# First attention of a gated cross-attention network: TensorE's groups put in another order within each sequence's eight ticks

## The chip, the cores and the metric

The kernel runs on one core of one Trainium2 chip. The metric is device time in microseconds (us) of one execution, smaller is better. Three executions were timed, and one more was profiled. A measurement of this kernel can tell a change of about 1% from none.

## What is computed

There are 64 sequences of 128 tokens and 256 channels, and a context of the same shape. Four layers follow each other: a first attention, a first feed-forward layer (ternary weights), a second attention and a second feed-forward layer. The change touches the first attention alone:

```python
qh, kh, vh = (z.reshape(B, S, 16, 16) for z in (layernorm(x), ctx, ctx))   # 16 heads of 16
s1 = einsum('bshe,bthe->bhst', qh @ wq1, kh @ wk1) / 4
s2 = einsum('bshe,bthe->bhst', qh @ wq2, kh @ wk2) / 4
attn = softmax(s1) - gain * softmax(s2)
o = einsum('bhst,bthe->bshe', attn, vh @ wv)
o = (o - mean(o)) / sqrt(var(o) + 1e-5)         # over each head's 16 channels
x = x + tanh(g_xattn[0]) * (o @ wo.T)
```

## The kernel before

The five engines run one program each, written out by hand. `Attention0.pe`, `act`, `dve`, `pool` and `sp` hold one loop each over ticks, eight to a sequence: `b, u = divmod(tick, 8)` (GpSimd's loop goes by whole sequences). Every engine executes its list strictly in order and waits on semaphores, so the place of a step in the list sets what stands behind it. `ahead(tick)` calls steps of the next layer, from tick 500 on.

One sequence b passes through these steps. The names of the program, the line on which the profile puts them and, for TensorE, the tile form of the matmul (contraction rows * output columns of the array) are:

- `turn_queries(b, half)`, L549, 128*128: four transposes of the normalised queries into bank 7. ScalarE's `q_stack` (L684) copies them out.
- `keys(p)`, L523, 64*128, and `values(p)`, L536, 128*128: once for each pair p of sequences, into banks 6 and 7. ScalarE's `k_high` (L664), VectorE's `rest_keys` (L757) and twelve DMAs of SyncE (`stack_keys`, two halves r of six) build the key stack; ScalarE's `values` (L670) builds `v_pad`.
- `maxima(b, u)`, L561, 48*128, u = 0 to 3: scores of four of the sixteen heads, two row tiles at once, into banks 0 and 1. VectorE's `find_max` (L764) reduces them. The next `maxima` waits for that (`max`).
- `max_rows(b)`, L510, 128*32: one transpose of the maxima into bank 6. ScalarE copies it (L690), and two DMAs of SyncE (L438) put it into the query stack as rows. `scores_t` waits for their landing (`s_mdma`).
- `scores_t(b, u)`, L574, 50*128: the transposed scores less the maxima, into banks 2 and 3. ScalarE's two `exponential`s (L695) read them; the next `scores_t` waits for both (`exp`).
- `weighted(b, u)`, L585, 128*32: weighted sums of the values, four column tiles at once, into bank 5. ScalarE's `out_t` (L700) copies each half of a sequence out.
- `back(b, hf)`, L602, 128*128: four transposes into bank 4. VectorE divides (L771, L774) and, after the second half, makes the `difference` (L781); GpSimd squares (L861), VectorE sums (`variance`, L786), GpSimd normalises (L867 to L871).
- `project(b)`, L612, and `project2(b)`, L619, 128*128: two transposes and two matmuls, again in bank 4; ScalarE's `normed_t` (L705) lies between them and VectorE's `add` (L791) ends the sequence.

Before, TensorE's list for one tick pair is: `maxima`, `weighted`, then (in u = 2) `max_rows`, and (u = 2, 4) a half of `turn_queries`; in the odd tick `scores_t`, then one of `back`, `project`, `back` with `values` or `keys`, `project2`. In the letters of the tile forms (M `maxima`, S `scores_t`, both with half the rows; W `weighted`, quarter columns; F full tile; K `keys`, half the rows) a sequence is

```
before:  M W | S F(back) | M W F(max_rows, turn) | S F(project) | M W F(turn) | S F(back, values) or F(back) K | M W | S F(project2)
after:   S M | W W F(project2) | S M | F(max_rows, turn, back) | S M (K) | W W F(project, values) | S M | F(turn, back)
```

The banks are the same in both: each group has one buffer in PSUM, so the next group of its kind waits for the engine that reads it.

Of the kernel before, what the change touches and what calls it, by code (L numbers as in the profile page):

```python
# [303 lines left out]
class Attention0:  # L304
# [77 lines left out]

    def stack_keys(self, w, p, r):

        s, k = self.s, p % self.NK
        w.wait_ge(s["k_lo"], 2 * p + r + 1)
        w.wait_ge(s["k_hi"], 2 * p + r + 1)
# [22 lines left out]
    def sp(self, w, ahead):  # L410
# [42 lines left out]
        for tick in range(self.START, self.END):  # L453
# [30 lines left out]
    def pe(self, w, ahead):  # L484
# [54 lines left out]
        def turn_queries(b, half):  # L539
# [5 lines left out]
            elif half == 0 and b % 2 and b + 1 < NSEQ:  # L545
# [7 lines left out]
        def maxima(b, u):  # L553
            n = 4 * b + u
            w.wait_ge(s["q_st"], 2 * b + 2)
# [35 lines left out]
        def back(b, hf):  # L591
            w.wait_ge(s["o_sb"], 2 * b + hf + 1)
            if b == 0:
                w.wait_ge(s["div"], 2 * hf)
            elif hf:
                w.wait_ge(s["n_sb"], b)
            elif b == 1:
                w.wait_ge(s["div"], 4)
            else:
                w.wait_ge(s["x_new"], b - 1)  # L600
# [4 lines left out]
        def project(b):  # L605
            w.wait_ge(s["pool"], 4 * b + 4)
            if b + 1 < NSEQ:
                w.wait_ge(s["div"], 4 * b + 6)
            else:
# [12 lines left out]
        for tick in range(self.START, self.END):  # L622
            b, u = divmod(tick, 8)
            o, v = divmod(tick - 4, 8)
            if u % 2 == 0:
                if 0 <= b < NSEQ:
                    maxima(b, u // 2)
                if 0 <= tick - self.LAG - 4 < 8 * NSEQ:
                    weighted(*divmod((tick - self.LAG - 4) // 2, 4))
                if u == 2 and 0 <= b - 1 < NSEQ:  # L630
                    max_rows(b - 1)
                if u in (2, 4) and 0 <= b + 1 < NSEQ:
                    turn_queries(b + 1, u // 2 - 1)
            else:
                if 0 <= tick - self.LAG < 8 * NSEQ:
                    scores_t(*divmod((tick - self.LAG) // 2, 4))
                if v == 1 and 0 <= o - 3 < NSEQ:
                    back(o - 3, 1)
                if v == 3 and 0 <= o - 4 < NSEQ:
                    project2(o - 4)  # L640
                if v == 5 and 0 <= o - 2 < NSEQ:
# [1611 lines left out]
```

## Time and profile before

| | |
|---|---|
| median of three executions | 1447.42 us (1446.23, 1447.42, 1459.62) |
| profiled execution, first to last instruction | 1446.3 us |
| first attention in it, `maxima` of the first sequence to those of the last | 45.0 to 739.3 us |
| TensorE busy, 100 to 700 us | 100% |
| VectorE, ScalarE, GpSimd busy, 300 to 400 us | 81.4, 74.3, 65.2 us of 100 |

The profiled execution's span is 1.1 us below the median; no other time of that execution is given, so the span stands for it. Matmuls are pipelined: a matmul of the profile lasts some 0.27 us, while the next starts 0.11 us after it. So TensorE's share of busy time says only that it never stood still, and what a group costs is read from its start to the start of the group after it. Neighbouring instructions of VectorE and ScalarE overlap in the records by some 0.1 us, and are read the same way.

### The profile page before, as it was taken

What the parts mean: (1) busy time and instruction counts of PE and PEld (TensorE: products, weight loads), DVE (VectorE), ACT (ScalarE), POOL (GpSimd) and SP (SyncE); (2) the same over time, 40 slices, a digit from 0 to 9 for tenths busy, and PEclk for the clock granted to TensorE, in tenths of its full rate; (3) what the DMA queues carried; (4) which work ended last, traced back from release to release, by engine and by line L of the source; (5) the groups of instructions that cost most, each with busy time, mean ns of one, the idle gap of its engine ahead of it and who ended that gap; (6) DMA issues with size and microseconds to landing.
All of it is one profiled execution on the core that took longest, in us unless ns stands there. A gap on an engine that the chain in (4) does not pass through costs nothing.

```text
span 1446.3 us, 30872 instructions
## 1 busy us (share of the span) xinstructions
PE 1327.5 (92%) x11617; PEld 896.8 (62%) x11672; DVE 1163.6 (80%) x1888; ACT 1050.8 (73%) x1739; POOL 769.1 (53%) x1225
## 2 busy tenths in 40 slices
PE   4799999999999999999997999999889988579898
PEld 3466666666666666666654666666667666434376
DVE  3577887887888878877786999998656899979988
ACT  2377777777777777777764988888745665689897
POOL 2156666767668667675767333441302586878100
PEclk9999999999999999999987999999999998889999
DMA  9666867758668576676530000000255463229099
GB/s 151 112 127 110 132 114 132 133 97 150 107 122 136 99 144 112 108 124 105 90 98 1 1 1 1 1 1 1 70 157 149 105 163 96 51 122 401 1 379 377
DMA packets 124964, 165.71 MB, mean 115 GB/s; under 512 B 47362, under 2 KB 78210, under 8 KB 120450
## 3 DMA queue, kind: packets, MB, share of 16 engines
q1 hardware_dynamic: 124048, 162.95, 49.8%
q8 instruction: 93, 1.52, 0.5%
q10 hardware_dynamic: 768, 0.79, 0.5%
q14 instruction: 55, 0.45, 0.1%
HBM read 76.07 MB, written 35.65 MB: 77 GB/s over the span
## 4 chain that ended last, share of the span: by engine, by line
PE 64%; DVE 13%; ACT 11%; issue 4%; POOL 4%; DMA 2%; SPq 1%; ACTq 0%; DVEq 0%; POOLq 0%
PE psum L574 10%; PE psum L585 10%; PE psum L561 7%; PE psum L602 5%; PE psum L549 4%; PE psum L619 4%; PE psum L982 4%; PE psum L1013 3%; ACT f_gelu L2071 3%; PE psum L1005 3%; ACT f_gelu L2063 2%; PE psum L523 2%; PE psum L536 2%; POOL a_fac L1772 2%; PE psum L612 2%
## 5 line engine op out<-in xcount | busy, mean ns | idle before, releaser
L764 DVE TENSOR_REDUCE neg_max<-psum 128x8 f32<-128x1024 f32 x256 | 313.1, 1223 | 67.9 <-PE psum L561 63.2
L695 ACT ACTIVATE exp_t<-psum 128x512 f32<-128x512 f32 x512 | 281.5, 597 | 49.6 <-PE psum L574 49.5
L869 POOL TENSOR_TENSOR rs<-rs,minus_half 128x16 f32<-128x16 f32 x64 | 186.4, 2912 | 5.0
L574 PEld LDWEIGHTS psum<-q_stack,k_stack 50*128 50x128 f32 x2048 | 135.0, 188 | 77.5 <-issue 73.2
L574 PE MATMUL psum<-q_stack,k_stack 50*128 50x128 f32 x2048 | 171.1, 287 | 0.8 <-ACT exp_t L695 0.8
L585 PE MATMUL psum<-exp_t,v_pad 128*32 128x256 f32 x2048 | 165.8, 396 | 0.0
L561 PE MATMUL psum<-k_stack,q_stack 48*128 48x256 f32 x1024 | 133.4, 339 | 14.9 <-DVE neg_max L764 11.3
L700 ACT ACTIVATE o_t<-psum 128x512 f32<-128x512 f32 x128 | 76.7, 599 | 89.9 <-PE psum L585 89.8
L861 POOL TENSOR_TENSOR sq<-u 128x256 f32<-128x256 f32 x64 | 39.3, 614 | 171.6 <-DVE u L781 170.6
L982 PE MATMUL psum<-f_w,f_xqt 128*128 128x512 bf16 x481 | 117.0, 383 | 6.9 <-DVE f_hid L1118 3.7
L561 PEld LDWEIGHTS psum<-k_stack,q_stack 48*128 48x128 f32 x1024 | 80.6, 188 | 66.9 <-issue 48.5
L684 ACT ACTIVATE q_stack<-psum 128x512 fp32r<-128x512 f32 x128 | 75.0, 586 | 51.8 <-PE psum L549 51.8
L90 DVE BATCH_NORM_STATS2 norm_stats<-x_state 128x6 f32<-128x256 f32 x256 | 102.8, 414 | 11.1 <-DMA x_state<-in_x 11.0
L1118 DVE SCALAR_TENSOR_TENSOR f_hid<-psum,f_sup,f_act 128x1024 f32<-128x1024 f32 x64 | 81.8, 1279 | 20.5 <-ACT f_act L1054 17.6
L1772 POOL TENSOR_TENSOR a_fac<-a_fac,a_expo 128x16 f32<-128x16 f32 x16 | 52.8, 3300 | 84.0 <-DVE a_fac L1678 83.5
L602 PE MATMUL psum<-ident,o_t 128*128 128x128 f32 x512 | 84.8, 289 | 0.7 <-DVE x_state L791 0.7
L549 PE MATMUL psum<-ident,q_nat 128*128 128x128 f32 x512 | 83.2, 287 | 0.7 <-ACT q_stack L684 0.7
L982 PEld LDWEIGHTS psum<-f_w,f_xqt 128*128 128x128 bf16 x512 | 49.9, 99 | 54.4 <-DVE f_hid L1118 5.9
L1068 ACT ACTIVATE f_hqt<-psum 128x1024 bf16<-128x1024 f32 x64 | 65.6, 1024 | 23.8 <-PE psum L1005 23.8
L771 DVE RECIPROCAL z_inv<-psum 128x16 f32<-128x16 f32 x128 | 32.6, 255 | 59.5 <-PE psum L602 59.5
L1123 DVE TENSOR_REDUCE f_hmax<-f_hid 128x1 f32<-128x1024 f32 x64 | 78.1, 1220 | 2.2
L619 PE MATMUL psum<-wo,o_nt 128*128 128x256 f32 x256 | 74.9, 417 | 3.6 <-DVE u L774 3.6
(232 smaller groups left out, 3078.8 us busy)
## 6 DMA issues: line engine op xcount, KB each, us to landing
k_stack<-k_hi SPq DMA_DIRECT2D x252, 128.0 KB, 4.7
g_scratch<-f_gelu SPq DMA_DIRECT2D x18, 1024.0 KB, 4.7
k_stack<-k_lo SPq DMA_DIRECT2D x126, 128.0 KB, 5.0
f_gelu<-g_scratch SPq DMA_DIRECT2D x12, 1024.0 KB, 11.5
ctx_t<-in_ctx_t SPq DMA_DIRECT2D x32, 256.0 KB, 5.3
x_state<-in_x SPq DMA_DIRECT2D x16, 512.0 KB, 7.0
v_in<-in_ctx SPq DMA_DIRECT2D x32, 256.0 KB, 5.6
v_scratch<-v_in SPq DMA_DIRECT2D x32, 256.0 KB, 5.4
```

What stands on the lines that cost most here:

```text
L90: w.e.bn_stats(self.stats[:, k % 2, b % 16], self.x[:, b, :]).then_inc(n["moments"], 1)
L549: r = e.transpose(psum[:, 7, n * P:(n + 1) * P], self.q_nat[:, 2 * pair:2 * pair + 2, :].rearrange("p h c -> p (h c)"), ident[:, :])
L561: r = e.matmul(psum[:, j, o:o + D], self.q_st[rows, b % self.NQ, pair, :], self.k_st[rows, b // 2 % self.NK, pair // 2 % 2, pair % 2, :, p ...
L574: r = e.matmul(psum[:, 2 + j, o:o + P], self.k_st[rows, b // 2 % self.NK, pair // 2 % 2, pair % 2, i, pair // 4, b % 2, :], self.q_st[rows ...
L585: r = e.matmul(psum[32 * i:32 * i + 32, 5, (u % 2) * D:(u % 2) * D + D], self.v_pad[:, (b // 2) % 2, b % 2, 4 * u + i, :], self.prob[:, n ...
L602: r = e.transpose(psum[:, 4, n * P:(n + 1) * P], self.o_t[:, hf].rearrange("p u w t -> p (u w) t")[:, n, :], ident[:, :])
L619: r = e.matmul(psum[:, 4, 0:D], self.o_nt[:, b % 2, h, :], self.wo[:, h, :], start=h == 0, stop=h == 1)
L695: e.activation(self.prob[:, n % 3, j].rearrange("p n w t -> p (n w t)"), psum[:, 2 + j, :], ACT.Exp).then_inc(s["exp"], 1)
L764: e.tensor_reduce(self.negm[:, b % 2, :, :, 2 * u:2 * u + 2].rearrange("p j w n -> p j n w"), psum[:, 0:2, :].rearrange("p j (n w k) -> p ...
L869: e.tensor_tensor(self.rs[:, i], self.rs[:, i], self.expo[:, :], ALU.pow).then_inc(s["pool"], 1)
L982: r = e.matmul(psum[:, bank + h, :], self.xqt[:, b % 2, c, :], weights[:, c, h * BANK:(h + 1) * BANK], start=c == 0, stop=c == 1)
L1118: e.scalar_tensor_tensor(out=self.hid[:, b % self.HS], in0=psum[:, 2:4, :].rearrange("p j c -> p (j c)"), scalar=self.s_up[:, b:b + 1], in ...
```

## The change

TensorE's steps are the same instructions in another order (second line of the letters above): `scores_t` and `maxima` stand together in each even tick, `weighted` comes in twos in ticks 1 and 5, full-tile steps share ticks 3 and 7 or follow the `weighted`s. ScalarE's and VectorE's lists are put in an order to match, GpSimd's `square` and `normalise` move behind `normed_queries` and the sums, SyncE stacks the second half of the keys (r = 1) first. Several waits name another count, since bank 4 now goes round as back(1), project, back(0), project2. No instruction that computes or moves data is added or taken away. (The sums of ticks show that `scores_t(b, 0)` now stands five ticks behind `max_rows(b)`, seven before.)

```diff
+    def turned(self, p, r):
+
+        return 2 * p + (r + 1 if p < 2 else 2 - r)
...
-        w.wait_ge(s["k_lo"], 2 * p + r + 1)
-        w.wait_ge(s["k_hi"], 2 * p + r + 1)
+        w.wait_ge(s["k_lo"], self.turned(p, r))
+        w.wait_ge(s["k_hi"], self.turned(p, r))
         w.wait_ge(s["st_pe"], 8 * (p - self.NK + 1) - 1 + r)
...
-            if (tick + 18) % 16 == 0 and (tick + 18) // 16 < NSEQ // 2 and (tick + 18) // 16 != 1:
-                self.stack_keys(w, (tick + 18) // 16, 0)
+            if tick == -18:
+                self.stack_keys(w, 0, 0)
+            if (tick + 16) % 16 == 0 and 2 <= (tick + 16) // 16 < NSEQ // 2:
+                self.stack_keys(w, (tick + 16) // 16, 1)
             if (tick + 12) % 16 == 0 and 2 <= (tick + 12) // 16 < NSEQ // 2:
-                self.stack_keys(w, (tick + 12) // 16, 1)
+                self.stack_keys(w, (tick + 12) // 16, 0)
...
-                w.wait_ge(s["q_st"], 4 * p - 2)
+                w.wait_ge(s["q_st"], 4 * p - 3)
...
-            elif half == 0 and b % 2 and b + 1 < NSEQ:
+            elif half and b % 2 == 0 and b + 2 < NSEQ:
                 w.wait_ge(s["k_lo"], b + 3)
...
         def maxima(b, u):
             n = 4 * b + u
-            w.wait_ge(s["q_st"], 2 * b + 2)
+            w.wait_ge(s["q_st"], 2 * b + 1 + u // 2)
...
         def back(b, hf):
             w.wait_ge(s["o_sb"], 2 * b + hf + 1)
+            if hf == 0 and b >= 2:
+                w.wait_ge(s["n_sb"], b - 1)
+            elif hf == 0:
+                w.wait_ge(s["div"], 4 * b)
+            elif b >= 2:
+                w.wait_ge(s["x_new"], b - 1)
             else:
-                w.wait_ge(s["x_new"], b - 1)
+                w.wait_ge(s["div"], 4 * b + 2)
...
         def project(b):
             w.wait_ge(s["pool"], 4 * b + 4)
+            w.wait_ge(s["div"], min(4 * b + 8, 4 * NSEQ))
+            if b + 1 == NSEQ:
                 w.wait_ge(s["x_new"], b)
...
         def project2(b):
             w.wait_ge(s["n_sb"], b + 1)
-            w.wait_ge(s["div"], min(4 * b + 8, 4 * NSEQ))
+            if b + 2 < NSEQ:
+                w.wait_ge(s["div"], 4 * b + 10)
...
         for tick in range(self.START, self.END):
             b, u = divmod(tick, 8)
             if u % 2 == 0:
+                if 0 <= b - 2 < NSEQ:
+                    scores_t(b - 2, u // 2)
                 if 0 <= b < NSEQ:
                     maxima(b, u // 2)
+                if u == 4 and b % 2 and 0 <= b + 3 < NSEQ and b != -1:
+                    keys((b + 3) // 2)
+            elif u == 1:
+                if 0 <= b - 3 < NSEQ:
+                    weighted(b - 3, 2)
+                    weighted(b - 3, 3)
+                if 0 <= b - 5 < NSEQ:
+                    project2(b - 5)
+            elif u == 3:
+                if 0 <= b - 1 < NSEQ:
                     max_rows(b - 1)
-                if u in (2, 4) and 0 <= b + 1 < NSEQ:
-                    turn_queries(b + 1, u // 2 - 1)
+                if 0 <= b + 1 < NSEQ:
+                    turn_queries(b + 1, 0)
+                if 0 <= b - 3 < NSEQ:
+                    back(b - 3, 1)
+            elif u == 5:
+                if 0 <= b - 2 < NSEQ:
+                    weighted(b - 2, 0)
+                    weighted(b - 2, 1)
+                if 0 <= b - 4 < NSEQ:
+                    project(b - 4)
+                if b % 2 == 0 and 0 < b < NSEQ:
+                    values(b // 2)
             else:
+                if 0 <= b + 1 < NSEQ:
+                    turn_queries(b + 1, 1)
+                if 0 <= b - 2 < NSEQ:
+                    back(b - 2, 0)
+            if tick == -13:
+                keys(1)
+            if tick == -9:
+                values(0)
...
+            if u == 0:
+                if 0 <= b < NSEQ:
+                    q_stack(b, 1)
+                if 0 <= b + 1 < NSEQ:
+                    q_high(b + 1)
+            if u % 2 == 0 and 0 <= b - 2 < NSEQ:
+                exponential(4 * (b - 2) + u // 2, 0)
+                exponential(4 * (b - 2) + u // 2, 1)
...
+            if tick == -3:
+                values(0)
+            if u == 1 and 0 <= b - 3 < NSEQ:
+                out_t(b - 3, 1)
+            if u == 3:
                 if 0 <= b - 1 < NSEQ:
                     max_rows(b - 1)
                 if 0 <= b + 1 < NSEQ:
                     q_stack(b + 1, 0)
+            if u in (4, 5) and b % 2 and 0 <= b + 3 < NSEQ and b != -1:
+                k_high((b + 3) // 2, 5 - u if b > 0 else u - 4)
+            if u == 5:
+                if 0 <= b - 2 < NSEQ:
+                    out_t(b - 2, 0)
+                if 0 <= b - 4 < NSEQ:
+                    normed_t(b - 4)
             if u == 6 and b % 2 == 0 and 0 < b < NSEQ:
                 values(b // 2)
...
             if u % 2 == 0 and 0 <= b < NSEQ:
                 find_max(b, u // 2)
+            if u == 1:
+                if 0 <= b + 1 < NSEQ:
+                    rest_queries(b + 1)
+                if b % 2 == 0 and 4 <= b + 2 < NSEQ:
+                    rest_keys((b + 2) // 2, 0)
+                if 0 <= b - 5 < NSEQ:
+                    add(b - 5)
+            if u == 3 and 0 <= b - 3 < NSEQ:
+                divide(b - 3, 1)
+                difference(b - 3)
+            if u == 5:
+                if b % 2 and 4 <= b + 3 < NSEQ:
+                    rest_keys((b + 3) // 2, 1)
+                if 0 <= b - 5 < NSEQ:
+                    w.wait_ge(s["x_new"], b - 4)
+                    sh.moments(w, 1, b - 5)
+                if 10 <= b + 10 < NSEQ:
+                    sh.wait_x(w, (b + 10) // 8)
+                    sh.moments(w, 0, b + 10)
+            if u == 7:
+                if 0 <= b - 3 < NSEQ:
+                    variance(b - 3)
+                if 0 <= b - 2 < NSEQ:
+                    divide(b - 2, 0)
...
+            if 0 <= b - 6 < NSEQ - 8 and (b - 5) % 8 == 0:
+                sh.finish(w, 1, (b - 6) // 8)
             if 0 <= b + 2 < NSEQ:
                 normed_queries(b + 2)
             if 0 <= b - 3 < NSEQ:
-                normalise(b - 3)
+                square(b - 3)
             if b in self.CENTRE:
                 add_up(self.CENTRE.index(b))
             if b in self.CENTRE_END:
                 centre(self.CENTRE_END.index(b))
+            if 0 <= b - 3 < NSEQ:
+                normalise(b - 3)
```

The other waits of `back` and `project` follow the new round of bank 4; the removed lines of the loops stand in the kernel above. "..." marks what is left out.

## Rows read from the trace of the kernel before

**Rows 1.** Stretches: us, busy PE, PEld, DVE, ACT, POOL, granted clock, DMA share, GB/s.

```profile
300.00:400.00 100.00, 100.00 (x1000) 66.65 (x1001) 81.42 (x138) 74.27 (x150) 65.21 (x98) 1.00 0.70 123
...
740.00:760.00 20.00, 17.50 (x149) 10.18 (x141) 17.98 (x33) 10.74 (x21) 13.31 (x14) 0.77 0.36 118
```

**Rows 2.** TensorE's timeline from 300 us: start, duration, engine, line, operation, tiles, count.

```profile
300.99 0.51 PE L561 MATMUL psum<-k_stack,q_stack 48*128 48x256 f32 x4
301.43 0.64 PE L585 MATMUL psum<-exp_t,v_pad 128*32 128x256 f32 x8
302.00 0.66 PE L574 MATMUL psum<-q_stack,k_stack 50*128 50x128 f32 x8
302.59 0.66 PE L602 MATMUL psum<-ident,o_t 128*128 128x128 f32 x4
303.17 0.50 PE L561 MATMUL psum<-k_stack,q_stack 48*128 48x256 f32 x4
...
304.17 0.28 PE L510 MATMUL psum<-ident,neg_max 128*32 128x128 f32 x1
304.30 0.60 PE L549 MATMUL psum<-ident,q_nat 128*128 128x128 f32 x4
304.82 0.66 PE L574 MATMUL psum<-q_stack,k_stack 50*128 50x128 f32 x8
305.42 0.44 PE L612 MATMUL psum<-ident,u 128*128 128x128 f32 x2
305.79 0.51 PE L561 MATMUL psum<-k_stack,q_stack 48*128 48x256 f32 x4
...
307.97 0.66 PE L602 MATMUL psum<-ident,o_t 128*128 128x128 f32 x4
308.46 1.06 PE L536 MATMUL psum<-wv_bd,ctx_t 128*128 128x128 f32 x8
309.45 0.50 PE L561 MATMUL psum<-k_stack,q_stack 48*128 48x256 f32 x4
...
311.04 1.13 PE L619 MATMUL psum<-wo,o_nt 128*128 128x256 f32 x4
312.10 0.51 PE L561 MATMUL psum<-k_stack,q_stack 48*128 48x256 f32 x4
...
319.65 1.14 PE L523 MATMUL psum<-ctx_t,fold 64*128 64x256 f32 x8
...
320.96 0.64 PE L585 MATMUL psum<-exp_t,v_pad 128*32 128x256 f32 x8
...
322.12 1.13 PE L619 MATMUL psum<-wo,o_nt 128*128 128x256 f32 x4
```

**Rows 3.** Timelines of VectorE and ScalarE in that stretch, with what ended their idle time.

```profile
302.70 1.09 ACT L695 ACTIVATE exp_t<-psum 128x512 f32<-128x512 f32 x2 [0.57 <-PE psum L574]
304.24 1.21 DVE L764 TENSOR_REDUCE neg_max<-psum 128x8 f32<-128x1024 f32 x1
305.37 0.41 DVE L90 BATCH_NORM_STATS2 norm_stats<-x_state 128x6 f32<-128x256 f32 x1
306.33 1.23 DVE L764 TENSOR_REDUCE neg_max<-psum 128x8 f32<-128x1024 f32 x1 [0.55 <-PE psum L561]
```

**Rows 4.** The same, start of keys' copy (319 us) and a wait of TensorE (67 us).

```profile
320.84 0.60 ACT L664 ACTIVATE k_hi<-psum 128x512 fp32r<-128x512 f32 x1 [0.57 <-PE psum L523]
...
67.00 1.23 DVE L764 TENSOR_REDUCE neg_max<-psum 128x8 f32<-128x1024 f32 x1 [1.71 <-PE psum L561]
...
68.37 0.50 PE L561 MATMUL psum<-k_stack,q_stack 48*128 48x256 f32 x4 [0.25 <-DVE neg_max L764]
```

**Rows 5.** SyncE's timeline: the two DMAs of the maxima.

```profile
305.27 1.34 SPq L438 DMA_DIRECT2D q_stack<-max_rows  x2
```

**Rows 6.** The page, DMA issues: count, KB each, median us from issue to landing.

```profile
k_stack<-k_hi SPq DMA_DIRECT2D x252, 128.0 KB, 4.7
...
x_state<-in_x SPq DMA_DIRECT2D x16, 512.0 KB, 7.0
```

More of the change, by code:

```diff
@@ L623, in pe @@
             b, u = divmod(tick, 8)
-            o, v = divmod(tick - 4, 8)
             if u % 2 == 0:
+                if 0 <= b - 2 < NSEQ:
+                    scores_t(b - 2, u // 2)
                 if 0 <= b < NSEQ:
                     maxima(b, u // 2)
-                if 0 <= tick - self.LAG - 4 < 8 * NSEQ:
-                    weighted(*divmod((tick - self.LAG - 4) // 2, 4))
-                if u == 2 and 0 <= b - 1 < NSEQ:
-                    max_rows(b - 1)
-                if u in (2, 4) and 0 <= b + 1 < NSEQ:
-                    turn_queries(b + 1, u // 2 - 1)
-            else:
[L635 to L641, printed above, removed]
-                    back(o - 2, 0)
-                if v == 7 and 0 <= o - 3 < NSEQ:
-                    project(o - 3)
-                if tick == -13:
-                    keys(1)
-                if tick == -9:
-                    values(0)
-                if u == 5 and b % 2 and 0 <= b + 3 < NSEQ and b != -1:
-                    keys((b + 3) // 2)
-                if u == 5 and b % 2 == 0 and 0 < b < NSEQ:
-                    values(b // 2)
@@ L708, in act @@
             b, u = divmod(tick, 8)
-            o, v = divmod(tick - 4, 8)
-            if 0 <= tick - self.LAG - 1 < 8 * NSEQ:
-                exponential(*divmod(tick - self.LAG - 1, 2))
+            if u == 0:
[6 more added lines that the diff above has]
+                exponential(4 * (b - 2) + u // 2, 1)
             if tick == -16:
@@ L715, in act @@
                 k_high(1, tick + 12)
-            if u in (6, 7) and b % 2 and 0 <= b + 3 < NSEQ and b != -1:
-                k_high((b + 3) // 2, u - 6)
-            if u == 0:
-                if 0 <= b + 1 < NSEQ:
-                    q_high(b + 1)
-            if v in (2, 6) and 0 <= o - 2 < NSEQ:
-                out_t(o - 2, v // 4)
-            if u == 2:
+            if tick == -3:
[3 more added lines that the diff above has]
+            if u == 3:
                 if 0 <= b - 1 < NSEQ:
@@ L727, in act @@
                     q_stack(b + 1, 0)
-            if v == 0 and 0 <= o - 4 < NSEQ:
-                normed_t(o - 4)
-            if u == 4:
-                if 0 <= b + 1 < NSEQ:
-                    q_stack(b + 1, 1)
-            if tick == -3:
-                values(0)
+            if u in (4, 5) and b % 2 and 0 <= b + 3 < NSEQ and b != -1:
[5 more added lines that the diff above has]
+                    normed_t(b - 4)
             if u == 6 and b % 2 == 0 and 0 < b < NSEQ:
@@ L755, in rest_keys @@
             flat = lambda z: z[:, p % 2, r].rearrange("p h s k -> p (h s k)")
-            w.wait_ge(s["k_hi"], 2 * p + r + 1)
+            w.wait_ge(s["k_hi"], self.turned(p, r))
             e.tensor_tensor(flat(self.k_lo), psum[:, 6 + r, :], flat(self.k_hi).bitcast(F32),
@@ L836, in dve @@
                 sh.moments(w, 0, 8 + u // 4)
-            if u == 5 and 10 <= b + 10 < NSEQ:
-                sh.wait_x(w, (b + 10) // 8)
-                sh.moments(w, 0, b + 10)
             ahead(tick)
@@ L901, in pool @@
                 sh.finish(w, 0, (b + 9) // 8 + 1)
-            if 0 <= b - 5 < NSEQ - 8 and (b - 4) % 8 == 0:
-                sh.finish(w, 1, (b - 5) // 8)
-            if 0 <= b - 3 < NSEQ:
-                square(b - 3)
+            if 0 <= b - 6 < NSEQ - 8 and (b - 5) % 8 == 0:
+                sh.finish(w, 1, (b - 6) // 8)
             if 0 <= b + 2 < NSEQ:
```

28 lines of the change are left out of this document (removed).

## The prediction, made before the changed kernel ran

> **What bounds the kernel now.** I read the busy time by stretches first. From 100 to 700 us, of which one stretch is shown, TensorE is busy all the time at a granted clock of 1.00; VectorE is busy for 81.4%, ScalarE for 74.3%, GpSimd for 65.2% [rows 1]. So in the steady part of the first attention TensorE waits for nobody, and its list of instructions is the time. The timeline of TensorE then shows the price of each group, from its start to the start of the next. An even sequence goes from 300.99 to 312.10, that is 11.11 us; an odd one from 311.04 to 322.12, 11.08 us [rows 2]. I take 11.10. The timelines of the other engines give the delays between a group and its reader, which matter once TensorE is quicker [rows 3, 4].
>
> **What a group costs, and where.** [rows 2] has `maxima` at 0.44 (300.99 to 301.43), `weighted` 0.57, `scores_t` 0.59, `back` 0.58 before `maxima`, `max_rows` 0.13, the transposes of the queries after it 0.52, `project` 0.37, `project2` 1.06. The reader is to compare equal groups with unequal neighbours. Four transposes of `back` take 0.58 when `maxima` follow, but 0.49 (307.97 to 308.46) when `values`, of the same tile form, follow: leaving a form costs 0.09. Four transposes of queries take 0.52 when `max_rows` stands before them, against 0.58: entering costs 0.06. The eight matmuls of `values` with one exit take 0.99, so a matmul of 128 columns streams in (0.99 - 0.09) / 8 = 0.11. `scores_t` has four pairs, 0.44, and takes 0.59: again 0.15 for entry and exit. `weighted` has two quads of 256 columns, 2 x 0.22 = 0.44, and takes 0.57: 0.13. `maxima` has two pairs of 256 columns, 0.44, and takes 0.44: nothing, on the way from a full tile to the `weighted` of quarter columns. `keys` with the `maxima` behind them take 1.31 (319.65 to 320.96), six pairs at 0.22: within one form nothing is lost.
>
> **TensorE's sum after.** A sequence changes its tile form 18 times before and 10 times after (max_rows counted with the full tiles, since 0.13 is little more than 0.11).
> - `scores_t` and `maxima` together: (0.59 - 0.09) + 0.43 = 0.93, four times: 3.72. Toward `weighted` the exit is free, as now.
> - Toward a full tile (ticks 2 and 6) the trace has no `maxima`. Bounds are 0 (as toward `weighted`) and 0.09 (as `scores_t` toward `back`) each. Less than 0 is excluded, since the stream itself is counted at its clean rate. I take the middle, 0.09 for both, and keep 0 and 0.18.
> - `weighted` in twos: 2 x (0.57 + 0.44) = 2.02. `project2` 1.06.
> - Tick 3: 0.13 + (0.52 - 0.09) + (0.58 - 0.06) = 1.08. Tick 7: (0.58 - 0.09) + (0.58 - 0.06) = 1.01.
> - Tick 5: in an even sequence project and values (0.37 - 0.09) + 0.99 = 1.27; in an odd one project 0.37, and keys in tick 4, 1.31 - 0.43 = 0.88, together 1.25.
>
> The sum is 3.72 + 0.09 + 2.02 + 1.06 + 1.08 + 1.01 + 1.26 = 10.24, bounds 10.15 and 10.33; against 11.10 TensorE's own work falls by 0.86 a sequence.
>
> The Trainium skill ("TensorEngine Tiling (Array Packing)", Key Properties) says that a change of tiling mode, and not of the tile alone, drains TensorE. The trace agrees for most changes, 0.13 to 0.15 for a stay, but not for the way from `maxima` to `weighted`, which is free. At one price for all changes the sum would be lower than mine; that is the second rival below.
>
> **What is late next.** TensorE has been the cover of every other wait; it is now shorter, and the groups come in clumps. The closest pair of like groups is that of tick 6 and the next tick 0: 0.93 + 0.05 + 1.01 = 1.99 us.
> - Scores: 302.00 to 302.70 until the first exponential starts, 1.09 for two [rows 3], and 0.15 from a reader's end to the matmul that waits for it (68.37 - 67.00 - 1.23 = 0.14) [rows 4]: 1.94. It fits by 0.05.
> - Maxima: 305.79 to 306.33, 1.23, 0.15 [rows 2, 3]: 1.92. It fits by 0.07.
> - Odd sequences put `keys` into tick 4 and a chain on ScalarE behind them: 1.19 until the copy starts (319.65 to 320.84 [rows 2, 4]), two copies and `out_t`, `normed_t`, then the exponentials that the next tick 0 waits for. Two exponentials take 1.09 and one 0.60, so ScalarE starts one every 0.49 [rows 3]: 1.19 + 3 x 0.49 + 0.35 + 1.09 + 0.15 = 4.25. TensorE's own way from `keys` to that tick 0 is 0.88 + 1.01 + 0.37 + 0.93 + 0.05 + 1.01 = 4.25. It fits with nothing left. Were the copies 0.60 apart, it would be late by 0.4 in every second sequence, 0.2 a sequence.
> - VectorE: 81.4% of 11.10 is 9.04 us, or 88% of 10.24. Its `find_max` yields after 1.13 (304.24 to 305.37 [rows 3]). A wait on its list now stops `find_max`, and with it `maxima` and all that stands behind them on TensorE. Walking through a pair with these steps, I find each `find_max` done before the next `maxima` is due, by 0.1 us at the closest, that of tick 6. ScalarE is at 8.25 of 10.24, GpSimd at 7.24; GpSimd's `normalise` now waits behind the sums, but has until tick 5 of the next sequence.
> - SyncE: the two DMAs of the maxima take 1.34 to issue [rows 5]; the six of half the keys stay one before and one behind them. `scores_t` now stands five ticks behind `max_rows`, formerly seven. From tick 0: 3.00 to the next scores, 0.70 + 1.09 for exponentials before the copy, 0.3 for the copy, 1.34 for the issue, 0.15 to the matmul, 6.6 in all; so 3.6 us are left for the landing. The trace has no landing of these DMAs; the nearest, of 128 KB, take 4.7 from issue [rows 6], of which issuing is 0.7. I take it that 8 KB land sooner and cost nothing; the other end is the third rival.
>
> The margins of 0.00 to 0.07 will not all hold: I add 0.08 a sequence and get 10.32, with a range of 10.15 (no wait, both exits free) to 10.5 (the chain of `keys` 0.2 late).
>
> Scores run beside maxima for sequences 2 to 61, 60 times. 60 x (11.10 - 10.32) = 47 us. Start and end (sequences with no partner) have the same groups as before. From 740 to 760 TensorE waits for 2.5 us and its clock falls to 0.77, 4.6 us worth of clock [rows 1]; the new round of bank 4 can make that better or worse: -4 to +4, taken as 0. The profiled execution becomes 1446.3 - 47 = 1399; the median stood 1.1 above it: 1400.
>
> **The rivals.**
> - Forecast: 60 x 0.95 to 60 x 0.6 saved, 1390 to 1411. Chance 0.62.
> - Waits pile up. ScalarE's and VectorE's copies don't overlap where each waits for another group, and one late `find_max` in tick 6 also delays the transposes that VectorE needs. For it: margins of nothing at two places, a VectorE at 88%. Against: today's schedule, in strict order too, has no wait of TensorE at all. At 10.5 to 10.9 a sequence it gives 1411 to 1435, near 1422. Chance 0.17.
> - Every change of tile form costs the same 0.15, 8 fewer save 1.2: 9.9. The loop of scores then holds tick 6 to tick 0 at 1.94, so 10.0 and 1446.3 - 66 = 1380, 1381 as a median. Against it stands the free step to `weighted`. Chance 0.09.
> - Slower: the maxima's DMAs land late. If they queue behind the keys' and take between 4.7 and 7.0 us [rows 6], 5.85, the loop is 3.00 + 1.79 + 0.3 + 0.7 (first issue) + 5.85 + 0.15 = 11.8 a sequence: 60 x 0.7 = +42, 1489. It decides from 5.2 us on. Against: today too they are issued right behind half of the keys' (305.27 [rows 5]), and TensorE never waits for them. Chance 0.06.
> - The change doesn't do what it says: the price belongs to the groups, not to their neighbours, or comes back between `scores_t` and `maxima`. Then 11.0 to 11.1, 1441 to 1447. The two prices of `back` speak against it. Chance 0.06.
>
> **How the numbers follow.** The likeliest gives 1400. For 8 in 10 the range takes the forecast whole (0.62), two thirds of the piling waits and half or more of the lower rival: 1383 to 1427. A change of 1%, 14.5 us, is about what can be told from none. Faster than 1433: 0.62 + 0.09 + 0.16 = 0.87; within: 0.08 (the last rival and an edge of the second); slower: 0.05 (most of the fourth).
>
> **What would show it.** In the profile after: `scores_t` followed by `maxima` at 0.50; two `weighted`s at 1.01; `maxima` before `max_rows` or `turn_queries` between 0.43 and 0.52; a pair of sequences at 20.6 us. TensorE still busy for over 98% in the steady part; the waits that appear should be `scores_t` on ScalarE and `maxima` on VectorE, in the tick 0 behind `keys`. VectorE at 88%, ScalarE at 80%. The forecast is wrong if TensorE is idle for more than 0.3 us a sequence there, if its clock falls below 1.00 in these waits, or if `scores_t` waits for a DMA.

## The result, and the profile after

The changed kernel takes 1387.1 us (median of four executions, 1385.16 to 1391.49), the kernel before 1448.92 beside it (1446.23 to 1459.62): a ratio of 0.957, interval 0.955 to 0.960. That is 13 us less than the 1400 forecast, inside the range. The profiled execution has a span of 1383.3 us, 63.0 below that of before.

Where the 63 us went is read by anchors, the first `maxima` of a sequence. Up to sequence 4 the kernel gains 1.4 us; from sequence 4 to sequence 60 the way shrinks from 621.7 to 564.7 us, 57.0 or 1.02 a sequence; from there to the last `maxima` 2.7; to the last `add` of the layer 2.0. The other three layers take 652.8 and 653.0 us. So all of it lies in the first attention, nearly all in the steady part. (The first `maxima` of all start at 28.1 us before and at 27.7 after; the 45.0 in the table of the kernel before is the fourth group of the first sequence.)

TensorE's timeline of the kernel after, sequence by sequence as in [rows 2]:

```profile
301.02 0.66 PE L580 MATMUL psum<-q_stack,k_stack 50*128 50x128 f32 x8
301.52 0.46 PE L567 MATMUL psum<-k_stack,q_stack 48*128 48x256 f32 x4
301.91 0.28 PE L516 MATMUL psum<-ident,neg_max 128*32 128x128 f32 x1
...
303.50 0.45 PE L567 MATMUL psum<-k_stack,q_stack 48*128 48x256 f32 x4
303.88 1.07 PE L591 MATMUL psum<-exp_t,v_pad 128*32 128x256 f32 x16
...
306.14 0.66 PE L580 MATMUL psum<-q_stack,k_stack 50*128 50x128 f32 x8
...
308.07 0.66 PE L580 MATMUL psum<-q_stack,k_stack 50*128 50x128 f32 x8
308.54 0.48 PE L567 MATMUL psum<-k_stack,q_stack 48*128 48x256 f32 x4
308.95 1.07 PE L591 MATMUL psum<-exp_t,v_pad 128*32 128x256 f32 x16
309.95 1.13 PE L625 MATMUL psum<-wo,o_nt 128*128 128x256 f32 x4
...
313.48 0.46 PE L567 MATMUL psum<-k_stack,q_stack 48*128 48x256 f32 x4
313.78 1.03 PE L529 MATMUL psum<-ctx_t,fold 64*128 64x256 f32 x8
314.74 0.64 PE L591 MATMUL psum<-exp_t,v_pad 128*32 128x256 f32 x8
```

Read from start to start, `scores_t` takes 0.50 (it was 0.59), `maxima` behind it 0.39 toward a full tile (301.52 to 301.91), 0.38 (tick 4) or 0.41 (tick 0) toward `weighted`, 0.30 toward `keys` (it was 0.44 for itself), two `weighted`s 1.00 (twice 0.57). From the scores of tick 6 to those of the next tick 0 is 308.07 - 306.14 = 1.93, the length of 1.94 that the prediction worked out for this loop; TensorE is held up there for some 0.03. A quiet pair of sequences takes 19.95 us, 9.98 a sequence, where [rows 2] had 22.19. The mean of 27 pairs is 20.16: eleven of them are longer, up to 21.1.

What these pairs wait for shows in the waits of 100 to 660 us (us in total, times, longest), of which I show those of TensorE and of GpSimd's chain:

```profile
POOL rs L884 <- DVE var L801: 70.2, 41, 3.2
...
PEld psum L580 <- ACT exp_t L708: 9.3, 56, 0.2
...
PEld psum L529 <- DMA ctx_t<-in_ctx_t: 5.7, 10, 1.1
```

`keys` (L529) wait for a transfer, that of the context, in about every third pair. For one of them SyncE's row, the load's time from issue to landing, and TensorE's row:

```profile
329.38 0.59 SPq L435 DMA_DIRECT2D ctx_t<-in_ctx_t  x1
```

```profile
DMA to landing us min/median/max: 4.4/4.4/4.4
```

```profile
333.78 1.14 PE L529 MATMUL psum<-ctx_t,fold 64*128 64x256 f32 x8
```

The load is issued at 329.38, right behind the last of the twelve transfers of the key stack, lands 4.4 later, at 333.78, and `keys` start in that moment. Before, the load stood at the same place of the list. One such load of the kernel before, and its time to landing:

```profile
310.98 0.59 SPq L431 DMA_DIRECT2D ctx_t<-in_ctx_t  x1
```

```profile
DMA to landing us min/median/max: 5.6/5.6/5.6
```

It landed at 316.6, and `keys` began at 319.65 [rows 2]: 3.1 us of slack. From the load's tick to that of `keys` it was seven ticks of 1.39 us, 9.7; it is six of 1.25 now, 7.5, since `keys` went from tick 5 to tick 4. That takes 2.2 of the slack. The rest goes because SyncE is further behind TensorE: `keys` begin 5.3 us after the issue in an even-running pair (308.46 to 313.78), 2.2 less than the six ticks, where it was 1.0 less than the seven. Two stretches of the kernel after, to be held against [rows 1]:

```profile
300.00:400.00 100.00, 99.26 (x1098) 72.56 (x1094) 86.90 (x149) 79.19 (x164) 73.19 (x114) 1.00 0.72 139
680.00:700.00 20.00, 17.90 (x140) 11.78 (x141) 16.09 (x31) 9.49 (x19) 14.64 (x18) 0.68 0.31 98
```

TensorE is still the bound, with VectorE at 87%, ScalarE at 79%. Near the end of the layer the granted clock is again lower, 0.68 from 680 to 700.

### The profile page after: what moved, and what is told of

The parts are those of the page before. It is cut to its first block, busy times and chain, and to the rows that moved or that the text cites. A ratio compares the mean times of both kernels' runs of the same rounds, so it can differ in the third digit from the quotient of the medians.

```text
span 1383.3 us, 31084 instructions
## 1 busy us (share of the span) xinstructions
PE 1265.6 (91%) x11672; PEld 891.4 (64%) x11672; DVE 1152.2 (83%) x1888; ACT 1036.0 (75%) x1739; POOL 768.3 (56%) x1225
## 4 chain that ended last, share of the span: by engine, by line
PE 54%; DVE 14%; ACT 12%; DMA 5%; issue 5%; POOL 4%; SPq 4%; ACTq 0%; DVEq 0%; POOLq 0%
PE psum L580 9%; PE psum L591 8%; PE psum L625 4%; PE psum L567 4%; PE psum L999 4%; DMA ctx_t<-in_ctx_t 4%; PE psum L555 4%; PE psum L1030 3%; ACT f_gelu L2088 3%; PE psum L1022 3%; PE psum L608 3%; SPq L396 3%; ACT f_gelu L2080 3%; PE psum L529 2%; POOL a_fac L1789 2%
## 5 line engine op out<-in xcount | busy, mean ns | idle before, releaser
L591 PE MATMUL psum<-exp_t,v_pad 128*32 128x256 f32 x2048 | 139.6, 391 | 0.0
L567 PE MATMUL psum<-k_stack,q_stack 48*128 48x256 f32 x1024 | 119.5, 308 | 15.3 <-DVE neg_max L779 12.1
L999 PE MATMUL psum<-f_w,f_xqt 128*128 128x512 bf16 x512 | 123.6, 383 | 7.0 <-DVE f_hid L1135 5.9
L90 DVE BATCH_NORM_STATS2 norm_stats<-x_state 128x6 f32<-128x256 f32 x256 | 98.4, 413 | 11.5 <-DMA x_state<-in_x 11.5
L713 ACT ACTIVATE o_t<-psum 128x512 f32<-128x512 f32 x128 | 77.9, 609 | 16.7 <-PE psum L591 16.7
L591 PEld LDWEIGHTS psum<-exp_t,v_pad 128*32 128x32 f32 x2048 | 53.9, 110 | 45.6 <-issue 11.1
L608 PE MATMUL psum<-ident,o_t 128*128 128x128 f32 x512 | 78.4, 277 | 0.0
L1078 ACT ACTIVATE f_hr<-f_hid,f_hscale 128x1024 f32<-128x1024 f32 x64 | 73.6, 1149 | 0.0
```

What stands on the lines that cost most here:

```text
L90: w.e.bn_stats(self.stats[:, k % 2, b % 16], self.x[:, b, :]).then_inc(n["moments"], 1)
L567: r = e.matmul(psum[:, j, o:o + D], self.q_st[rows, b % self.NQ, pair, :], self.k_st[rows, b // 2 % self.NK, pair // 2 % 2, pair % 2, :, p ...
L591: r = e.matmul(psum[32 * i:32 * i + 32, 5, (u % 2) * D:(u % 2) * D + D], self.v_pad[:, (b // 2) % 2, b % 2, 4 * u + i, :], self.prob[:, n ...
L608: r = e.transpose(psum[:, 4, n * P:(n + 1) * P], self.o_t[:, hf].rearrange("p u w t -> p (u w) t")[:, n, :], ident[:, :])
L999: r = e.matmul(psum[:, bank + h, :], self.xqt[:, b % 2, c, :], weights[:, c, h * BANK:(h + 1) * BANK], start=c == 0, stop=c == 1)
```

## The experiments

Each kernel is the changed one with the edit shown, or, for two, the kernel before. Every time is given with its ratio to the kernel before, measured beside it, whose median was 1448 to 1449 us.

**One form more for `weighted`.** `w_apart` puts a full-tile group between the two `weighted`s.

```diff
                     weighted(b - 3, 2)
-                    weighted(b - 3, 3)
                 if 0 <= b - 5 < NSEQ:
                     project2(b - 5)
+                if 0 <= b - 3 < NSEQ:
+                    weighted(b - 3, 3)
... (tick 5 likewise: weighted, project, weighted, values)
```

> The changed kernel, with the two weighted sums of ticks 1 and 5 parted by project2 and project (weighted, project2, weighted; weighted, project, weighted). Two more changes of tile form in each sequence, nothing else. Theory A (what is saved is the price of changing the form, 0.13 to 0.15 us each): a sequence takes 0.26 to 0.30 us more, 16 to 18 us in all, 1403 to 1405 us. Rival B (the gain came from the new order of the waits and the other engines' lists): spreading the weighted sums changes little, 1383 to 1391 us.

Measured: 1411.7 us (1406.35 to 1413.77), 0.974 (0.972 to 0.977); 24.6 more than the changed kernel. A quiet pair takes 20.89, 0.94 more.

```profile
308.66 0.66 PE L580 MATMUL psum<-q_stack,k_stack 50*128 50x128 f32 x8 [0.16 <-ACT exp_t L710]
...
309.54 0.64 PE L591 MATMUL psum<-exp_t,v_pad 128*32 128x256 f32 x8
310.10 1.13 PE L625 MATMUL psum<-wo,o_nt 128*128 128x256 f32 x4
311.17 0.64 PE L591 MATMUL psum<-exp_t,v_pad 128*32 128x256 f32 x8
311.73 0.44 PE L580 MATMUL psum<-q_stack,k_stack 50*128 50x128 f32 x4
```

Tick 1 goes from 309.54 to 311.73, 2.19 instead of 2.06: 0.13 for the stay more, the same 0.57 for one `weighted` as before. In the even sequences tick 5 grows by 0.33, since there the second `weighted` now also parts `project` from `values`. Together the forms cost 0.74 of the 0.94. The other 0.2 is a wait, 0.16 in the first row: `out_t` comes a group later on ScalarE, and holds up the exponentials for the next `scores_t`. The price of a form is confirmed, but the expectation of 16 to 18 us was a third too low: it counted two changes a sequence where an even one has three more, and left this wait out.

**One form more between `scores_t` and `maxima`.** `s_m_apart` puts a half of `turn_queries` between them in tick 6.

```diff
                     scores_t(b - 2, u // 2)
+                if u == 6 and 0 <= b + 1 < NSEQ:
+                    turn_queries(b + 1, 1)
                 if 0 <= b < NSEQ:
                     maxima(b, u // 2)
... (and out of tick 7)
```

> The changed kernel, with the second half of the transposed queries moved from tick 7 to between scores and maxima in tick 6: scores, turn, maxima, back instead of scores, maxima, turn, back. Two more changes of form in each sequence. Theory A: 0.59 + 0.59 + 0.43 + 0.59 = 2.20 us instead of the 1.94 measured, 0.26 us a sequence, 16 us in all, 1403 us. Rival B: no change by more than 4 us, since nothing is waited for longer.

Measured: 1421.94 us (1420.27 to 1422.82), 0.982 (0.980 to 0.983), 34.8 more than the changed kernel where 16 was expected. TensorE, its weight loads (PEld) and VectorE's `find_max`, in tick 6 to 0:

```profile
301.31 0.66 PE L555 MATMUL psum<-ident,q_nat 128*128 128x128 f32 x4
...
301.90 0.50 PE L567 MATMUL psum<-k_stack,q_stack 48*128 48x256 f32 x4
...
302.44 1.23 DVE L779 TENSOR_REDUCE neg_max<-psum 128x8 f32<-128x1024 f32 x1 [1.69 <-PE psum L567]
...
303.72 0.30 PEld L567 LDWEIGHTS psum<-k_stack,q_stack 48*128 48x128 f32 x4 [0.29 <-DVE neg_max L779]
```

The groups cost what the sum says: 0.59, 0.59 (301.31 to 301.90), 0.43 and 0.59 until the scores of the next tick at 302.92. But the `maxima` of tick 6 now start 0.6 later, at 301.90, and those of tick 0 would follow 1.5 later; they come at 303.72, 1.82 after, when `find_max` has read the bank (0.29 of idle time in the last row). The pair is 1.35 longer; the forms, 0.28 a sequence, are 0.56 of it, and this wait, 0.3 to 0.4 a sequence, is most of the rest. A form change that moves a group within its loop costs the form and the loop.

**Order within the merged pair.** `m_before_s` runs `maxima` ahead of `scores_t`.

```diff
-                if 0 <= b - 2 < NSEQ:
-                    scores_t(b - 2, u // 2)
                 if 0 <= b < NSEQ:
                     maxima(b, u // 2)
+                if 0 <= b - 2 < NSEQ:
+                    scores_t(b - 2, u // 2)
```

> The changed kernel, with maxima ahead of scores in the even ticks. The number of changes of form is the same, but a stay now ends with scores. Theory A (maxima pay for entry and exit as all others do, and their pairs stream at 0.11 us): the two together take 0.88 us as now, the time stays within 5 us of 1387. Rival C (the prediction's reading: the pairs of maxima stream at 0.22 us and leaving from them is free): 0.43 + 0.53 = 0.96 us, 0.08 us for each of four pairs, 0.32 us a sequence, 19 us more, 1406 us.

Measured: 1392.29 us (1390.97 to 1394.81), 0.962 (0.960 to 0.964).

```profile
309.36 0.50 PE L567 MATMUL psum<-k_stack,q_stack 48*128 48x256 f32 x4
309.70 0.56 PE L580 MATMUL psum<-q_stack,k_stack 50*128 50x128 f32 x8
310.20 0.66 PE L555 MATMUL psum<-ident,q_nat 128*128 128x128 f32 x4
310.31 1.08 ACT L708 ACTIVATE exp_t<-psum 128x512 f32<-128x512 f32 x2 [1.20 <-PE psum L580]
...
311.56 0.64 PE L580 MATMUL psum<-q_stack,k_stack 50*128 50x128 f32 x8
...
319.42 0.51 PE L567 MATMUL psum<-k_stack,q_stack 48*128 48x256 f32 x4
320.05 1.21 DVE L779 TENSOR_REDUCE neg_max<-psum 128x8 f32<-128x1024 f32 x1
...
321.41 0.50 PE L567 MATMUL psum<-k_stack,q_stack 48*128 48x256 f32 x4
```

Here `maxima` take 0.34, `scores_t` 0.49, 0.83 together against 0.89. So `maxima` take 0.34 even with no exit, far below the 0.44 that I had given their stream. The quiet pair stays at 19.95, but in two unequal halves. An even sequence takes 9.76 instead of 9.99: behind `maxima` the exponentials start 0.61 after `scores_t` (309.70 to 310.31), not 0.70, and the scores of ticks 6 and 0 stand 1.86 apart (309.70 to 311.56). So the 1.93 of the changed kernel is no floor: it belongs to the order in which `scores_t` enter the form. An odd sequence takes 10.19 where nothing waits for the context (10.19 in `ctx_first_ms` below, which has the same order): `keys` take 1.06 behind `scores_t` instead of 0.96, and in tick 0 `maxima` wait for a `find_max` that starts 0.63 after its `maxima` (319.42 to 320.05; 0.55 in the even sequence) and ends at 321.26, 0.15 before they start, the delay of [rows 4]. The 5 us above the changed kernel are more waits of `keys` for the context: 13.3 us on their weight loads from 100 to 660 us, where the changed kernel has 5.7.

**The stream of `maxima` by itself.** `m_twice` issues each of its matmuls twice. It repeats work and changes nothing in what is computed.

```diff
-            for pair in (2 * u, 2 * u + 1):
+            for pair in (2 * u, 2 * u + 1) * 2:
```

> The changed kernel, with each group of maxima issuing its four matmuls twice (the same values written twice). Theory A: a pair of 256 columns costs 0.12 us within one form, so 0.23 us for each group, 0.93 us a sequence, about 58 us in all, 1445 us. Rival C: 0.22 us a pair, 0.44 us a group, 1.75 us a sequence, about 109 us in all, 1496 us.

Measured: 1435.01 us (two executions, 1434.77 and 1435.25), 0.991 (0.989 to 0.993).

```profile
305.90 0.69 PE L567 MATMUL psum<-k_stack,q_stack 48*128 48x256 f32 x8
306.52 1.07 PE L591 MATMUL psum<-exp_t,v_pad 128*32 128x256 f32 x16
```

`maxima` go from 0.385 to 0.616: two pairs more cost 0.231, 0.116 a pair. I had read 0.22 a pair off the `keys`, whose matmuls are as wide. Eight times 0.231 is 1.85 a pair of sequences, and a quiet pair grew by 1.84. Thirty pairs make 55 us; `keys` no longer wait for the context (7 us back); 48 was measured. This settles the step: 0.44 was never the stream of `maxima`, it was 0.23 of stream and 0.21 around it.

**The changed kernel again.** `after_again` tests how steady the time is; it adds an empty line.

```diff
+
```

> The changed kernel once more, beside the next three on the same chip: 1385 to 1390 us.

Measured: 1387.0 us (1385.91 to 1389.49), 0.958 (0.957 to 0.959); the mean pair is 20.22.

**The wait for the context.** `ctx_first` stacks the first half of the keys two ticks later, behind the context's load in SyncE's list.

```diff
-            if (tick + 12) % 16 == 0 and 2 <= (tick + 12) // 16 < NSEQ // 2:
-                self.stack_keys(w, (tick + 12) // 16, 0)
+            if (tick + 10) % 16 == 0 and 2 <= (tick + 10) // 16 < NSEQ // 2:
+                self.stack_keys(w, (tick + 10) // 16, 0)
```

> The changed kernel, with SyncE's stacking of the first half of the keys (r = 0, six DMAs of 128 KB) two ticks later, behind the load of the context that the next keys need, instead of ahead of it. In the trace after, keys start 0.04 to 0.05 us behind the landing of the context in the pairs that take longer than 19.95 us. Theory D (these landings cost 20.16 - 19.95 = 0.21 us a pair): no pair waits, 6 us less than the changed kernel, 1380 to 1382 us. Rival E (the chain from keys through ScalarE to the next scores is as late, and takes over): less than 2 us less.

Measured: 1379.83 us (1376.99 to 1380.9), 0.952 (0.951 to 0.954). It is, with the next one, the quickest version, 7 us below the changed kernel, and outside that one's spread. SyncE's list, then the stretch of 100 to 640 us (columns as in [rows 1]):

```profile
304.99 0.34 SPq L435 DMA_DIRECT2D ctx_t<-in_ctx_t  x1
305.43 0.61 SPq L396 DMA_DIRECT2D k_stack<-k_hi  x1
```

```profile
100.00:640.00 540.00, 539.82 (x6007) 393.88 (x6006) 472.69 (x806) 433.52 (x891) 404.37 (x614) 1.00 0.70 133
```

From sequence 6 on every pair but two (20.21 and 19.90) takes 19.96 or 19.97 now, and no wait for the context is left. It was the cause of the uneven pairs.

**Both orders together.** `ctx_first_ms` adds `maxima` ahead of `scores_t` to `ctx_first`.

```diff
(the edits of ctx_first and of m_before_s)
```

> ctx_first, with maxima ahead of scores in the even ticks as well. With maxima first the two groups took 0.341 + 0.488 = 0.83 us instead of 0.88, but scores then waited. Theory F (what held that version back was the landing of the context): 0.05 us in the two or three ticks that no loop holds, 3 to 9 us less than ctx_first, 1373 to 1378 us. Rival E (the waits of scores for ScalarE take it all): as ctx_first, 1380 to 1382 us.

Measured: 1379.83 us (1375.58 to 1381.8), 0.952 (0.951 to 0.954), a pair 19.92. No gain: an even sequence takes 9.76, an odd one 10.19, for 9.99 and 9.97 in `ctx_first`. In the odd one `keys` take 1.06 behind `scores_t` where they took 0.96 behind `maxima`, and the `maxima` of tick 0 start 0.14 later for `find_max`. Why `keys` cost more there is open.

**GpSimd's order.** The prediction costed the move of `square` and `normalise` at nothing. `pool_old` puts both back as they were:

```diff
+            if 0 <= b - 3 < NSEQ:
+                square(b - 3)
             if 0 <= b + 2 < NSEQ:
                 normed_queries(b + 2)
             if 0 <= b - 3 < NSEQ:
-                square(b - 3)
+                normalise(b - 3)
... (add_up, centre)
-            if 0 <= b - 3 < NSEQ:
-                normalise(b - 3)
```

> The changed kernel with GpSimd's list in the order of before (square, normed_queries, normalise, then the sums of the values). Forecast: nothing on TensorE's path changes, within 3 us of the changed kernel. Rival G (GpSimd's order is part of the gain, since normalise ahead of the sums keeps the centring of the values, SyncE's stores and the DMAs behind them late): over 5 us slower.

`pool_norm` puts only `normalise` back ahead of the sums (`add_up`, `centre`), `square` stays behind `normed_queries`:

```diff
                 square(b - 3)
+            if 0 <= b - 3 < NSEQ:
+                normalise(b - 3)
... (add_up, centre)
-            if 0 <= b - 3 < NSEQ:
-                normalise(b - 3)
```

> The changed kernel with only one half of GpSimd's order undone: normalise stands ahead of the sums of the values again, normed_queries stay ahead of square. With both halves undone the kernel took 1397.5 us, and ScalarE waited 10.9 us for normed queries. Theory H (the normed queries behind square did it): within 3 us of the changed kernel, 1385 to 1390 us. Rival G (normalise ahead of the sums did it): 1395 to 1399 us.

Measured: `pool_old` 1397.51 us (1393.03 to 1398.21), 0.965 (0.964 to 0.966), 10.4 above the changed kernel; `pool_norm` 1409.94 us (1401.56 to 1412.62), 0.971 (0.968 to 0.975), 22.8 above. Both expectations were missed. A wait of `pool_old`, then those of `pool_norm`, 100 to 660 us:

```profile
ACT q_nat L690 <- POOL xn L127: 10.9, 12, 1.7
```

```profile
POOL rs L884 <- DVE var L801: 118.0, 53, 5.7
...
DVE var L801 <- POOL sq L878: 13.6, 11, 2.0
PEld psum L625 <- DVE u L789: 12.8, 11, 2.0
```

GpSimd is busy for 73% of the time, so none of its work is late by its amount; it is late by its place. With the old order ScalarE waits for the normalised queries (10.9 us). With `normalise` ahead of the sums GpSimd stands still for VectorE's `variance` (118 us against 70.2; with both moves undone it is 107.4) and does the sums afterwards, so `square` of the next sequence is late; VectorE waits for it (13.6), with `find_max` and the divisions queued behind, and `project2` waits for VectorE. It is worse than both moves undone, so the two belong together. Part of the 22.8 us is clock. From sequence 4 to 60 the kernel grew by 16.7, and two pairs of 24.8 and 24.4 us hold 9.0 of it. One of them has this wait of `project2`, and behind it this stretch (columns as in [rows 1]):

```profile
522.39 1.13 PE L625 MATMUL psum<-wo,o_nt 128*128 128x256 f32 x4 [1.48 <-DVE u L789]
```

```profile
524.00:531.00 7.00, 7.00 (x48) 5.04 (x49) 4.24 (x7) 3.95 (x8) 4.01 (x6) 0.51 0.16 43
```

TensorE is granted 0.5 of its clock, the lower level of 1.2 GHz, for 6.8 us behind this wait of 1.48, and for 6.8 us behind one of 1.14 at 597 us; at half speed that is some 3.4 us each time, more than the wait itself. Waits for the context of up to 1.1 in the changed kernel and 1.2 in `m_before_s` were not followed by such a stretch, so no rule for it is shown here. How the rest divides among the waits is not settled: TensorE's rows give 12.8 on the weight loads and 7.5 on the matmuls, in part the same time. The trace of `pool_old` is of its fastest execution, 1393.03, so it holds only a part of the 10.4.

**A part of the change in the kernel before.** If forms alone were the gain, `weighted` in twos there would give 3 x 0.14 a sequence, since `maxima` and `scores_t` also meet in one place. `before_w_twos` changes TensorE's list only:

```diff
                 if 0 <= tick - self.LAG - 4 < 8 * NSEQ:
-                    weighted(*divmod((tick - self.LAG - 4) // 2, 4))
+                    m = (tick - self.LAG - 4) // 2
+                    if m % 2:
+                        weighted(*divmod(m - 1, 4))
+                        weighted(*divmod(m, 4))
```

> The kernel before, with one edit of TensorE's list: the weighted sums of a half sequence stand together at the place of the second one, in ticks 2 and 6, none in ticks 0 and 4. No other engine's list changes. In tick 0 maxima are then followed by scores of the same form (two changes of form fewer), in tick 4 by the transposed queries (one fewer): 15 changes instead of 18 a sequence. Theory A: 3 x 0.14 = 0.42 us a sequence less, 25 us in all, 1422 to 1425 us. Rival B (the gain of the whole change came from the new lists of waits of all engines): within 4 us of 1448.

Measured: 1453.51 us (1449.79 to 1456.39), 1.002 (1.000 to 1.004): nothing gained. A quiet pair takes 22.23, for 22.19. In tick 7 to 1 of one sequence:

```profile
306.58 0.60 ACT L703 ACTIVATE o_t<-psum 128x512 f32<-128x512 f32 x1 [0.66 <-PE psum L585]
...
307.63 0.59 ACT L667 ACTIVATE k_hi<-psum 128x512 fp32r<-128x512 f32 x1
...
308.11 0.60 ACT L698 ACTIVATE exp_t<-psum 128x512 f32<-128x512 f32 x1
...
308.86 0.55 PE L574 MATMUL psum<-q_stack,k_stack 50*128 50x128 f32 x6 [0.27 <-ACT exp_t L698]
```

Two `weighted`s do take 1.00. But ScalarE has `out_t` and a copy of the keys around its exponentials, the second ends at 308.71, and `scores_t` waits 0.27. One early pair takes 26.7 us: there such a wait lasts 1.44, and the granted clock is at its lower level afterwards:

```profile
84.20:94.40 10.20, 10.20 (x63) 7.46 (x59) 3.86 (x7) 4.38 (x9) 3.90 (x9) 0.50 0.84 118
```

So `before_w_twos_act` has the same edit and moves those copies behind both exponentials of tick 7:

```diff
-            if u in (6, 7) and b % 2 and 0 <= b + 3 < NSEQ and b != -1:
-                k_high((b + 3) // 2, u - 6)
+            if u == 6 and b % 2 and 0 <= b + 3 < NSEQ and b != -1:
+                k_high((b + 3) // 2, 0)
+            if tick == -17:
+                k_high(0, 1)
+            if u == 0 and b % 2 == 0 and 0 < b < NSEQ - 2:
+                k_high((b + 2) // 2, 1)
+            if u == 0 and b % 2 and 0 < b - 1 < NSEQ:
+                values(b // 2)
...
-            if u == 6 and b % 2 == 0 and 0 < b < NSEQ:
-                values(b // 2)
```

> before_w_twos, and ScalarE's list changed in one more place: the copy of the values (tick 6) and the second copy of the keys (tick 7) come behind both exponentials of tick 7, where the trace of before_w_twos shows scores of tick 1 waiting 0.27 and 0.19 us for these exponentials. Theory A2 (fewer changes of form pay only once ScalarE's list lets the scores come): the waits of scores in tick 1 are gone and scores behind maxima enter without a price, 0.4 us a sequence less than before_w_twos, 24 us, 1426 to 1432 us. Rival B2 (fewer changes of form bring nothing in the order of before, whatever ScalarE does): within 4 us of before_w_twos, 1450 to 1458 us.

Measured: 1450.51 us (1447.2 to 1459.84), 1.002 (1.000 to 1.004). The second miss on the same question:

```profile
313.41 0.50 PE L561 MATMUL psum<-k_stack,q_stack 48*128 48x256 f32 x4
...
314.29 0.65 PE L602 MATMUL psum<-ident,o_t 128*128 128x128 f32 x4
315.24 0.50 PE L561 MATMUL psum<-k_stack,q_stack 48*128 48x256 f32 x4 [0.30 <-DVE neg_max L771]
```

The wait of the scores is gone, and another stands in its place: taking a `weighted` out of one tick pair brings two `maxima` closer together than their loop, and they wait for `find_max` until 1.83 after the first. The two cancel: over a sequence the groups are 0.43 cheaper (`weighted` 0.28, `maxima` 0.09, `scores_t` 0.06), `back` with the wait behind it lasts 1.00 on the mean where it lasted 0.59, and a quiet pair takes 22.17. In the old layout the `weighted`s are the distance between like groups.

## Why the prediction held, and where its numbers were off

- **The bound and its mechanism: right.** TensorE's list was the time, changes of form its waste, and both stay so: 18 changes fell to 10 and a quiet sequence from 11.10 to 9.98, 0.14 for each. `w_apart` and `s_m_apart` put single changes back and found them at 0.13 to 0.17. Most expected signs hold: `scores_t` at 0.50, two `weighted`s at 1.00, 99.3% busy where more than 98 was asked, VectorE 87% for 88, ScalarE 79% for 80. Three do not: the `maxima` are below the 0.43 to 0.52 given them, the pair is at 19.95 to 20.16, not 20.6, and the waits that count are those of `keys`.
- **The step that failed: `scores_t` with `maxima`, 3.72 + 0.09.** In the quiet pairs it measures 1.97 for the four `scores_t`, and 1.56 (even) or 1.47 (odd) for the four `maxima`: 3.48 on the mean, 0.33 less. The prediction gave `maxima` a stream of two pairs at 0.22 and a free way out, since 0.44 was then used up. `m_twice` shows 0.116 a pair, and the way out costs like others: 0.39 toward a full tile, 0.38 or 0.41 toward `weighted`, 0.30 where `keys` of the same form follow. With a change on both sides they took 0.44, so their stay in a form cost 0.14 like the rest. The bound "less than 0 is excluded" for the exits toward a full tile rested on that stream and was wrong: they came out 0.04 below the 0.43, not 0.045 above. Two rows could have told before: 0.11 for a `scores_t` pair of 128 columns is no evidence that 256 columns take twice that, and the 0.22 was taken from `keys`, groups with other operands.
- **The other terms of the sum: right within 0.02,** but for `keys`, 0.96 for 0.88, and tick 7, 1.05 for 1.01, of which 0.03 is the wait of the scores. `weighted` 2.00 for 2.02, tick 3 1.09 for 1.08, tick 5 1.26 for 1.27 (even). All of them make 9.99 (even) and 9.97 (odd) against 10.24.
- **The rule and the rival of one price.** The rival put every change at 0.15 and got 10.0 a sequence and 1381; it was 6 us off, the forecast 13. The Trainium skill ("TensorEngine Tiling (Array Packing)", Key Properties) says that changing the tiling mode drains TensorE, with no exception for a kind of matmul. The traces of the kernels here agree in so far as every change has its price, now for `maxima` too, though a drain as such is in no row; the exception that the prediction saw was a mis-read stream.
- **The loops: right for this order.** 1.94 for scores was met to 0.01 (1.93 in the quiet pair). It is not a floor: with `maxima` first (`m_before_s`, `ctx_first_ms`) it was 1.86, and what kept the pair at 19.92 to 19.95 were dearer `keys` and a late `find_max` in the odd sequences. The loop of maxima was put at 1.92; the waits of `s_m_apart` and `before_w_twos_act` end after 1.82 and 1.83, so that term was 0.1 too long.
- **The waits: the size right, the place wrong.** 0.08 a sequence was added for waits on exponentials and `find_max`; 0.10 came, but at `keys`, for the context. The prediction weighed SyncE's list for the maxima's DMAs alone, and never put the context's load, which stands in the same list, against `keys`, which move one tick forward in ticks that are shorter. `ctx_first` shows it: 7 us. So that the total of the waits came out right is luck.
- **Costs at nothing.** The new places on GpSimd were costed at nothing, as "it has until tick 5". In this layout they are worth 10 us together. That is no part of the difference between before and after; it is what the new order of TensorE would have cost with the old order of GpSimd.
- **Slower rival, late DMAs of maxima: did not come.** No wait of `scores_t` for them shows in the changed kernel.
- **Start and end at 0, and the count of 60:** `scores_t` stand beside `maxima` for sequences 2 to 63 (`scores_t(b - 2)` with `maxima(b)`, b up to 63), 62 times and not 60. That is 1.6 us more in the forecast. Beyond 60 sequences the span gained 2 us, so start and end themselves gave about 0.

From the sizes: 0.26 less in the sum and 0.02 more in waits, 60 times, is 14 us, and with 2 for what lies beyond the 60 sequences this is the 16 by which the span's gain of 63 exceeds the 47 forecast.

## What to carry to other kernels

Price a change of tile form on TensorE from pairs of equal groups with unequal neighbours, and take the stream of a group only from a row or a run in which the number of its own matmuls changes, not from another group of the same width. Fewer changes pay only as long as like groups stay as far apart as their loop through the reading engine is long: the whole order, in which like groups stand 1.9 or more apart, gave 62 us, and merging the weighted sums in the old layout gave nothing, twice. When TensorE's groups move, walk every other queue against them, the loads and GpSimd too: a load left behind six other transfers, when its reader moved forward, cost 7 us, GpSimd's old order 10. A wait of TensorE can cost more than it lasts, when the granted clock falls behind it.

## What the runs showed of the hardware

- Pairs of `maxima`, 48 rows by 256 columns in two row tiles at once, stream at 0.116 us, hardly more than the 0.11 of a pair or a matmul of 128 columns; `keys`, of the same width, need some 0.22 a pair (0.96 for four, less an exit of 0.09). What makes the difference, the weight load or the operands' type, was not tried.
- A stay in a form costs about the same, 0.13 to 0.17 for entry and exit, whether row halves, column quarters or the full array are entered. `maxima` lose another 0.06 that no order took away (0.30 where nothing changes behind them, 0.23 of stream).
- The order of groups of one form matters: `maxima` then `scores_t` 0.83, the other way 0.89; `keys` 0.96 behind `maxima`, 1.06 behind `scores_t`. The reason is open.
- Twice in `pool_norm` and once in `before_w_twos` a wait of TensorE of 1.1 to 1.5 us was followed by 6.8 to 10.2 us at a granted clock of 0.50 (1.2 GHz); other waits of 1.1 to 1.2 us were not.
